# Second layer's selective scans: where tile sums, the sum over n and the products with B are made

## What is computed

```
h[d, n] at t = exp(delta[d] * A[d, n]) * h[d, n] at t-1 + delta[d] * u[d] * B[n]
y[d] at t    = sum over n of h[d, n] * C[n]  +  Dp[d] * u[d]
```

## Time and profile before

| | |
|---|---|
| Median of 3 runs | 18,655.86 us (18,643.19 to 18,657.38) |
| Span of the profiled execution | 18,660.7 us |
| Stage of the second layer's scans in it | from 9030 to 16,229 us |
| PE, DVE, ACT, POOL busy over the whole span | 90%, 86%, 81%, 67% |
| DMA engines' busy share in the stage | 0.32 |

### The profile page before, as it was taken

How to read it: one execution, slowest core, us unless ns; L and a number is a source line. 1 busy time by engine, 2 the same in 40 slices (tenths; PEclk the granted TensorE clock), 3 DMA queues, 4 the chain that set the end, 5 groups by cost and what they waited for, 6 DMA issues and landing times. The chain is left out here.

```text
span 18660.7 us, 271066 instructions
## 1 busy us (share of the span) xinstructions
PE 16820.2 (90%) x78344; PEld 10186.0 (55%) x78344; DVE 16050.6 (86%) x12158; ACT 15162.6 (81%) x24326; POOL 12567.1 (67%) x6247
## 2 busy tenths in 40 slices
PE   8799998899996798879899999999999999989798
PEld 3355554455552364455566666666666666547374
DVE  3799998899996486479899999999999999879698
ACT  7699996799992555557899999999999999845556
POOL 0099993599990474135799999999999999700101
PEclk9899998899997899999999999999999999999899
DMA  5788886788879677777433333333333333441313
GB/s 175 230 242 245 236 250 208 233 246 237 247 223 249 217 224 222 253 237 277 166 113 112 113 112 119 113 112 113 112 112 114 122 113 113 125 138 54 104 53 101
DMA packets 898273, 3166.02 MB, mean 170 GB/s; under 512 B 145638, under 2 KB 180170, under 8 KB 872140
## 3 DMA queue, kind: packets, MB, share of 16 engines
q1 hardware_dynamic: 817612, 3011.91, 51.1%
q10 hardware_dynamic: 79104, 136.10, 2.4%
HBM read 2342.21 MB, written 805.32 MB: 169 GB/s over the span
## 5 line engine op out<-in xcount | busy, mean ns | idle before, releaser
L1788 DVE TENSOR_TENSOR_SCAN l1s_h<-l1s_da,l1s_pd 128x1024 f32<-128x1024 f32 x3072 | 6778.1, 2268 | 241.5 <-PE l1s_pd L1720 163.4
L1831 ACT ACTIVATE l1s_dm<-l1s_dut,l1s_bt 128x384 f32<-128x384 f32 x7424 | 4056.8, 604 | 74.0 <-PE l1s_pd L1720 73.8
L1814 ACT ACTIVATE l1s_da<-l1s_dl,l1s_a 128x1024 f32<-128x1024 f32 x3072 | 3496.9, 1138 | 32.0 <-DVE l1s_h L1788 31.0
L1720 PE MATMUL l1s_pd<-l1s_id,l1s_dm 128*128 128x128 f32 x22272 | 2967.8, 274 | 36.4 <-DVE l1s_h L1788 33.9
L1720 PEld LDWEIGHTS l1s_pd<-l1s_id,l1s_dm 128*128 128x128 f32 x22272 | 2561.9, 142 | 487.7 <-issue 287.9
L1694 POOL TENSOR_TENSOR l1s_pb<-l1s_h,l1s_cc 128x1024 f32<-128x1024 f32 x1024 | 2517.8, 2459 | 95.0 <-DVE l1s_h L1788 83.4
L1698 POOL TENSOR_TENSOR l1s_pa<-l1s_sm,l1s_cc 128x1024 f32<-128x1024 f32 x1024 | 2433.1, 2376 | 0.0
L1731 PE MATMUL l1s_py<-l1s_pb,l1s_both 128*128 128x512 f32 x4096 | 2157.4, 609 | 197.1 <-POOL l1s_pb L1694 197.1
L1689 POOL TENSOR_TENSOR l1s_sm<-l1s_h 128x1024 f32<-128x1024 f32 x928 | 2203.5, 2374 | 122.8 <-DVE l1s_h L1788 122.6
L1731 PE MATMUL l1s_py<-l1s_pa,l1s_id 128*128 128x512 f32 x4096 | 2113.4, 598 | 0.3 <-POOL l1s_pa L1698 0.3
L2654 POOL TENSOR_TENSOR l0sf_pr<-l0sf_h,l0sf_cc 128x1024 f32<-128x1024 f32 x768 | 1813.8, 2380 | 71.1 <-DVE l0sf_h L2736 54.8
(11 more groups left out here) (318 smaller groups left out, 30375.1 us busy)
## 6 DMA issues: line engine op xcount, KB each, us to landing
l1s_cc<-crows SPq DMA_DIRECT2D x1024, 512.0 KB, 3.7
l0sf_cc<-l0crowsf SPq DMA_DIRECT2D x512, 512.0 KB, 5.5
l0sb_cc<-l0crowsb SPq DMA_DIRECT2D x512, 512.0 KB, 5.5
l0sf_cc<-l0crowsf SPq DMA_DIRECT2D x512, 256.0 KB, 7.1
l0sb_cc<-l0crowsb SPq DMA_DIRECT2D x512, 256.0 KB, 7.1
dls<-l1p_dl SPq DMA_DIRECT2D x192, 512.0 KB, 7.0
duts<-l1p_dut SPq DMA_DIRECT2D x64, 1536.0 KB, 5.9
l1s_dut<-duts SPq DMA_DIRECT2D x64, 1536.0 KB, 7.2
```

What stands on the lines that cost most here:

```text
L1720: mm = pe.transpose(pd[:, s % 2, blk * 128:blk * 128 + 128], dm[:, rnd % 2, blk, j * 128:j * 128 + 128], idt[:, :])
L1788: dve.tensor_tensor_scan(h[:, s % 4, :], da[:, j, :], pd[:, s % 2, :], 0.0, ALU.mult, ALU.add)\
L1814: act.activation(da[:, j, :], dl[:, half, j, :], ACT.Exp, scale=a[:, HT * half + j, n:n + 1])\
L1831: ins = act.activation(dm[:, rnd % 2, blk, :], dut[:, half, blk, :], ACT.Identity, scale=bt[:, half, blk, n:n + 1])
```

## The change

Three parts of `l1_scans` are made in another way.
- The sum of tiles 0 and 1 is made by a transfer that POOL issues, from `h` to `h` in SBUF, with addition at its target (`accum_op`). POOL then multiplies `pb`, waits for the transfer, and multiplies `pa` from the same `h` slot. `sm`, POOL's 29 and DVE's 3 sums per image are gone; the ring `h` has six tiles. In the backward direction POOL writes the products reversed.
- `py` holds y time-major: each product is turned block by block (`is_transpose`, 8 blocks for `pb`, 8 for `pa`) and accumulated in PSUM. After the last round ACT copies `py` to SBUF (`hold`), PE turns it back (`back_b`, `back_a`; the former adds the halves of tile 2, 16 blocks), and DVE finishes as before. The adds of an image's first rounds come later, in rounds 2 and 3.
- Three of the eight blocks (5, 6, 7) are made with diagonals of B, for all 16 n; ACT multiplies the other five.

```diff
-    DIAGONAL = [n for n in range(N) if n % 2 == 0 or n % 4 == 3]
-    SUMS_ON_DVE = (6, 13, 25)
+    SCALED = 5
+    HALF_OF = (range(0, 3), range(3, SCALED))
+    STEP_BLOCKS = ((range(0, 1), range(1, 3), range(3, 5)), (range(0, 2), range(2, 4), range(4, 5)))
+    RING = 6
...
-                        if rnd == 3 and not first:
+                        if rnd == 4 and not first:
                             store(b - 1)
-                        if rnd == 4 and not first:
+                        if rnd == 5 and not first:
                             load(b, 1)
...
-                        if rnd not in SUMS_ON_DVE:
-                            pool.wait_ge(scan, nth(s + 1))
-                            pool.wait_ge(proda, nth(q - 2))
-                            pool.tensor_tensor(sm[:, rnd % 2, :], h[:, rnd * HT % 4, :], h[:, (rnd * HT + 1) % 4, :], ALU.add)\
-                                .then_inc(summed, 1)
+                        way = slice(None, None, -1 if rnd >= N else 1)
+                        low, other, high = (h[:, (rnd * HT + t) % RING, :] for t in range(HT))
+                        pool.wait_ge(scan, nth(s + 1))
+                        pool.sem_inc(begun, 1)
+                        pool.dma_start(low, other, accum_op=ALU.add).then_inc(s_sum[rnd % 2], 16)
                         pool.wait_ge(scan, nth(s + 2))
                         pool.wait_ge(s_cc[rnd % 4], b * (ROUNDS // 4 * 16) + rnd // 4 * 16 + 16)
                         pool.wait_ge(yb, nth(q - 2))
...
+                        pool.tensor_tensor(pb[:, rnd % 2, way], high, cc[:, rnd % 4, :], ALU.mult).then_inc(prodb, 1)
+                        pool.wait_ge(s_sum[rnd % 2], b * (ROUNDS // 2 * 16) + rnd // 2 * 16 + 16)
                         pool.wait_ge(ya, nth(q - 2))
...
+                        pool.tensor_tensor(pa[:, rnd % 2, way], low, cc[:, rnd % 4, :], ALU.mult).then_inc(proda, 1)
...
+                    pe.wait_ge(diagd, nth(b * N + (N - 1 if half else n)))
+                    for blk in range(SCALED, BLOCKS):
+                        pe.matmul(pd[:, s % 2, blk * 128:blk * 128 + 128], dut[:, half, blk, j * 128:j * 128 + 128],
+                                  bd[:, n, blk - SCALED, :], start=True, stop=True)
...
+                    for blk in range(BLOCKS):
+                        mm = pe.matmul(target[:, blk * 128:blk * 128 + 128], prods[:, rnd % 2, blk * 128:blk * 128 + 128], idt[:, :],
+                                       start=(rnd == 0 and blk % 4 == 0), stop=(rnd == ROUNDS - 1), is_transpose=True,
+                                       skip_group_check=True)
...
+                        if not first:
+                            if (rnd, j) == (0, 1):
+                                add_b(b - 1, ROUNDS - 1)
+                            if (rnd, j) == (0, 2):
+                                add_a(b - 1, ROUNDS - 1)
+                            if (rnd, j) == (1, 2):
+                                back_b(b - 1)
+                            if (rnd, j) == (2, 0):
+                                back_a(b - 1)
+                        if (rnd, j) == (2, 2):
+                            add_b(b, 0)
+                            add_b(b, 1)
+                        if (rnd, j) == (3, 0):
+                            add_a(b, 0)
+                        if (rnd, j) == (3, 1):
+                            add_a(b, 1)
+                        if rnd > 2 and j == 1:
+                            add_b(b, rnd - 1)
+                        if rnd > 2 and j == 2:
+                            add_a(b, rnd - 1)
...
                         if j == 0:
+                            dve.wait_ge(proda, nth(b * ROUNDS + rnd - 2))
+                        if j == 2:
                             dve.wait_ge(prodb, nth(b * ROUNDS + rnd - 2))
...
+                def hold(b, j, done, held):
+                    act.wait_ge(done, nth(b * ROUNDS + ROUNDS - 1))
+                    act.wait_ge(s_y[j], b * 16 + 16)
+                    act.activation(yo[:, j * HW:j * HW + HW], py[:, j, :], ACT.Identity).then_inc(held, 1)
```

More of the change, by code:

```diff
@@ L1600, in l1_scans @@
         cc = r.sb("cc", [128, 4, HW])
[L1601 to L1604, removed]
+        dm = r.sb("dm", [128, 2, SCALED, HT * 128])
+        da = r.sb("da", [128, 3, HW]); h = r.sb("h", [128, RING, HW])
+        pa, pb = (r.sb(n, [128, 2, HW]) for n in ("pa", "pb"))
+        yo = r.sb("yo", [128, 2 * HW + DHIGH])
         a = r.sb("a", [128, T, N]); dd = r.sb("dd", [128, 2, 4]); dsum = r.sb("dsum", [128, 2, 1])
-        bd = r.sb("bd", [128, len(DIAGONAL), 128])
-        idt, both = (r.sb(n, [128, 128]) for n in ("id", "both"))
+        bd = r.sb("bd", [128, N, BLOCKS - SCALED, 128])
+        idt = r.sb("id", [128, 128])
         pd = r.ps("pd", [128, 2, HW]); py = r.ps("py", [128, 2, HW])
@@ L1653, in store @@
                 def store(b):
-                    for j, fin in ((1, finb), (0, fina)):
+                    for j, rows, fin in ((1, slice(0, DHIGH), finb), (0, slice(0, DLOW), fina)):
                         sp.wait_ge(fin, nth(b))
                         sp.sem_inc(passed, 1)
-                        sp.dma_start(one(ys[:, j], b), yo[:, j, :]).then_inc(s_y[j], 16)
+                        sp.dma_start(one(ys[:, j, rows], b), yo[rows, j * HW:j * HW + HW]).then_inc(s_y[j], 16)
                 def body(b, first, final):
@@ L1718, in turn @@
                         for blk in blocks:
-                            if not (blk == LAST and diagonal(n)):
-                                mm = pe.transpose(pd[:, s % 2, blk * 128:blk * 128 + 128],
-                                                  dm[:, rnd % 2, blk, j * 128:j * 128 + 128], idt[:, :])
+                            mm = pe.transpose(pd[:, s % 2, blk * 128:blk * 128 + 128],
+                                              dm[:, rnd % 2, blk, j * 128:j * 128 + 128], idt[:, :])
                     mm.then_inc(trd, 1)
[L1724 to L1739, removed]
+                def add_y(b, rnd, prods, made, target, done, fin):
+                    pe.wait_ge(made, nth(b * ROUNDS + rnd))
+                    if rnd == 0:
+                        pe.wait_ge(fin, nth(b - 1))
+                    for blk in range(BLOCKS):
+                        mm = pe.matmul(target[:, blk * 128:blk * 128 + 128], prods[:, rnd % 2, blk * 128:blk * 128 + 128], idt[:, :],
+                                       start=(rnd == 0 and blk % 4 == 0), stop=(rnd == ROUNDS - 1), is_transpose=True,
+                                       skip_group_check=True)
+                    mm.then_inc(done, 1)
@@ new lines, in add_b, with add_a, back_b @@
+                def add_b(b, rnd):
+                    add_y(b, rnd, pb, prodb, py[:, 1, :], yb, finb)
+                def add_a(b, rnd):
+                    add_y(b, rnd, pa, proda, py[:, 0, :], ya, fina)
+                def back_b(b):
+                    pe.wait_ge(zeroed, nth(0))
+                    pe.wait_ge(heldb, nth(b))
+                    for blk in range(BLOCKS):
+                        for fold in range(2):
+                            at = blk * 128 + fold * DHIGH
+                            mm = pe.matmul(py[:, 1, blk * 128:blk * 128 + 128], yo[:, HW + at:HW + at + 128], idt[:, :],
+                                           start=(blk % 4 == 0 and fold == 0), stop=(fold == 1), is_transpose=True,
+                                           skip_group_check=True)
+                    mm.then_inc(backb, 1)
@@ L1741, in body, with back_a @@
+                def back_a(b):
+                    pe.wait_ge(helda, nth(b))
+                    for blk in range(BLOCKS):
+                        mm = pe.matmul(py[:, 0, blk * 128:blk * 128 + 128], yo[:, blk * 128:blk * 128 + 128], idt[:, :],
+                                       start=(blk % 4 == 0), stop=True, is_transpose=True, skip_group_check=True)
+                    mm.then_inc(backa, 1)
                 def body(b, first, final):
@@ L1745, in body @@
                             turn(b + (s + 1) // STEPS, (s + 1) % STEPS)
[L1746 to L1753, removed]
+                        if not first:
[18 more added lines that the diff above has]
+                            add_a(b, rnd - 1)
                 turn(0, 0)
                 images(pe, body)
[L1757 to L1760, removed]
+                add_b(IMAGES - 1, ROUNDS - 1)
+                add_a(IMAGES - 1, ROUNDS - 1)
+                back_b(IMAGES - 1)
+                back_a(IMAGES - 1)
             @block.vector
             def _(dve):
+                dve.memset(yo[:, 2 * HW:], 0.0).then_inc(zeroed, 1)
                 dve.wait_ge(s_w, ready)
@@ L1771, in _, with finish, finish_b, finish_a @@
                 dve.wait_ge(skipd, nth(2))
[L1773 to L1777, removed]
+                def finish(b, j, rows, back, fin):
+                    dve.wait_ge(back, nth(b))
```

(53 more changed lines are left out.)

26 lines of the change are left out of this document (7 added, 19 removed).

## The result

The changed kernel takes 21,856 us (median; 21,850 to 21,874) against 18,650 before: a ratio of 1.172, with an interval of 1.1704 to 1.1736. The forecast of 18,500 was wrong in sign and the range up to 19,700 too short; the mechanism is that of the first rival, above its highest price, 21,300. All of the difference lies in the second layer's scans: their stage took 10,403 us in place of 7199. One of the ten runs of a later experiment (e4) had a granted clock of 0.66 throughout in place of 0.95; it took 23,497 us and is left out of that experiment's ratio.

A forecast was written before the change was run, and what follows sets the result against it. Four engines were full together in the second layer's scans; DVE was to stay the bound. DVE busy 6836, idle 145 and image loads 60 gave 7041 against 7199 us, 158 less: 18,500, range 18,400 to 19,700.

The forecast's parts named there:

- the first rival: POOL's wait before pa: the transfer becomes the bound from 4.6 us of landing; kernel 18,760 to 21,300; chance 0.38.
- I take about 4, by the row nearest in size, place and stage: Landing of POOL's sum transfer: about 4 us, from a same-size C row's 3.7, so DVE stays the bound.
- The upper bound that stands just before it, 7.2: Sum's landing if a second operand (5.45) and a C row issued at the same event (another 1.75) both add.
- The thresholds: Sum's landing: within 4.3 us it hides under DVE's 6.70 per round; at 4.6 the round equals today's 7.03.
- The prediction charged the loads 60 us: Image loads sharing queues with the sums, twice per image: between nothing and 207 us, taken as 60.
- the needs of the engines: Second layer's scans, per round after the change: DVE 6.70, POOL 4.66, ACT 6.54 or 5.64 by direction, PE 5.36 us.
- the working's 0.22 and 0.109: PE's instruction times: 0.22 us for a diagonal block, 0.109 for a transpose, also taken for an accumulating turn.
- DVE's floor: DVE's need in the second layer's scans: 6.70 us per round, 6836 us busy in the stage.
- The sum's term of 60 us for DVE's waits on PE: DVE idle ended by PE in the second layer's scans: shrinks from 163 to about 60 us.
- The clock: Rival at PE: at 1.2 GHz its 5.36 us per round doubles to 10.7, kernel 22,400; chance 0.02.

The follow-up runs named there:

- e4: Changed kernel, but POOL multiplies pa one round later, behind the next transfer's issue, with eight ring tiles; 18,697 us, 1.0023 of the kernel before.
- e6: e4 with PE's adds of pa and pb exchanged, and adds, hold and finish at an image's head spread; 18,341 us, 0.9845 of the kernel before.
- e1: Changed kernel with only the sums undone: POOL and DVE add in place as before; 18,618 us, 0.9986 of the kernel before.
- e2: Changed kernel with C rows after the first four rounds loaded for only 16 of 1024 columns; 19,949 us, one run.
- e3: Changed kernel with the transfer copying tile 1 over tile 0 in place of adding; 19,992 us, one run.
- e5: Changed kernel with both the copying transfer and C rows of 16 columns after the first four rounds; 18,753 us, one run.

## Why the prediction was wrong, step by step

**The step that failed** is "I take about 4, by the row nearest in size, place and stage". The landing was 7.3 us. The upper bound that stands just before it, 7.2, came out nearly right: the second operand costs 1.4 to 1.5 us (5.8 against 7.3, 3.9 against 5.3) and the C row 1.9 to 2.0 (5.3 against 7.3, 3.9 against 5.8). For leaving out the second operand I gave two reasons: that the C row comes from DRAM, and that two of its 3.7 us are not movement. The first gained nothing, as the plain copy from SBUF without C rows lands in 3.9; the second is beside the point, as start and tail have to be paid here as well. For leaving out the C row I gave no reason at all, and the sum was to stand behind it. So 4 left nothing for two costs that the prediction had named.

**The thresholds** (4.3 us for DVE to set the pace, 4.6 to break even) are borne out in part. At a median of 5.3 the kernel is 7% slower. At 3.9 it should have been faster than before, and was 0.6% slower: the rounds are not alike, and those with long landings (the mean is 4.3, the longest 10.1) still stand on them. A threshold for one round is not one for the median.

**The first rival's price** was low: 7.2 us gave 21,300. The median of 7.3 leaves out the tail, and POOL's mean from issue to pa is 0.61 + 2.64 + 4.54 = 7.8 us. Of the landings' excess over their median, 485 us in all, some 330 lie in rounds 4, 5, 6, 20 and 21 of the images, in which, or right before which, y is stored and images are loaded; the longest, 12.2 us, is one of them. The prediction charged the loads 60 us. The other 155 lie in rounds without loads, and why they last longer no run shows. The range ended at 19,700 although the bound gave 21,300: with both extra costs named, leaving them 0.15 was the error of the chances.

**Right:** the needs of the engines, in the main. POOL's pa costs 2.35 us in both directions; only pb, right behind the issue, takes 2.64. From start to start in e6, three diagonals take 0.76 us, five transposes 0.55 and eight turns into y 0.87; by the working's 0.22 and 0.109 they would be 0.66, 0.55 and 0.87. DVE's floor was read well enough that e6, with the three parts of the change, comes out below the forecast of 18,500: the parts were sound, the place of one wait and the order of PE's adds were not. The sum's term of 60 us for DVE's waits on PE was too low as PE's order stood: they are 195 us in e1 and 373 in e4, and 50 only in e6.

**The clock** fell to 0.85 in the stage, yet not by the mechanism of that rival: e6 has the same turns and diagonals at a granted clock of 1.00. In the round shown above PE stood still for 2.1 us before its turns of pa, and the granted clock was 0.50, the lower of its two levels, from these turns on, and 1.00 again from 12056.5. From run to run it goes with PE's waits for pa: 0.85 where they are 2722 us in all, 0.93 and 0.92 in e2 and e3 with 1417 and 1363, 0.97 in e5 with 349. So the lower level most likely came from PE's waiting, though no run changes that alone; and POOL's chain shows that it did not set the time.

## What to carry to other kernels

When an operation is handed to a transfer, price the landing as start, movement of every operand that is read, all that is issued at the same event, and tail; then compare it with the work that is really queued ahead of its wait (here 3.25 us of issue and pb, against 7.3). A transfer that another queue issues at the same event can go first, even when it is issued a little later. If the landing doesn't fit, the cure is cheap: wait one round later, with two more tiles in the ring, which here took a loss of 17% down to 0.2% (e4). And after a late wait has been moved, look at the in-order engines behind it: here moving PE's adds, and the hold and finish at an image's head, was worth another 350 us (18,697 to 18,341) and made a gain of 1.6% of it.

## What the runs showed of the hardware

- A 512 KB sum of SBUF into SBUF costs all 16 DMA engines 2.7 us, a copy 1.3. With C rows of 16 columns beside them (image loads still ran in places) they land in 5.3 and 3.9 us, median; with whole C rows issued 3.5 us behind it, the sum lands in 4.9.
- A 512 KB load that SP issues 0.28 us behind POOL's sum moves ahead of it: the sum's first packet comes 3.4 us after its issue, against 1.5 us with C rows of 16 columns (medians).
- The product right behind an issue starts 0.61 us after the issue's start, behind a sum as behind a copy; but the issue's record lasts 0.87 us for the sum against 0.59, and the product takes 2.64 us behind a sum against 2.37 behind a copy.
- The same turns and diagonals ran at a granted clock of 0.85 where PE waited in nearly every round, and of 1.00 where it hardly did: the lower clock here looks like a symptom.
